# Values of four units multiplied together instead of two, with the maxima placed anew around them

## The reference

```python
def layer0(t):                      # t: (4, 1024, 768), normalised
    q, k, v = heads(t @ Wq + bq), heads(t @ Wk + bk), heads(t @ Wv + bv)
    attn = q @ k.T / 8 + rel_bias_h(q) + rel_bias_w(q)
    return (softmax(attn) @ v) @ Wp + bp
def layer1(t):                      # keys of the 7x7 neighbourhood only
    q, k, v = split(t @ qkv_w.T)
    return (softmax(q @ k[idx].T / 8) @ v[idx]) @ out_w.T
x = x + layer0(group_norm(x))
x = x + layer1(group_norm(x))
```

## Time and profile before

| | |
|---|---|
| median of three runs | 3558.11 us (3554.99 to 3559.51) |
| profiled execution | 3561.12 us, span 3558.6 us |
| PE busy | 3329.2 us, 94% |
| DVE, ACT, POOL busy | 46%, 34%, 30% |
| PE clock, mean granted | 0.989 of full |
| attention of the first image, layer 0 | 222 to 537 us of the span |
| attention of the first image, layer 1 | 782 to 857 us of the span |

### The profile page before, as it was taken

One profiled execution on the slowest core, in us unless ns is written; L12 is line 12 of the kernel. 1 busy time (PEld: TensorE's weight loads), 2 busy tenths in 40 slices (PEclk: granted clock), 3 DMA queues, 4 the chain that ended last, 5 costly groups with the idle time before them and its releaser, 6 DMA issues.

```text
span 3558.6 us, 49198 instructions
## 1 busy us (share of the span) xinstructions
PE 3329.2 (94%) x21388; PEld 2389.1 (67%) x21388; DVE 1639.5 (46%) x1497; ACT 1196.4 (34%) x1301; POOL 1083.5 (30%) x617
## 2 busy tenths in 40 slices
PE   6998899999999889999999888999989988899998
PEld 5864457786786455778678545587767854458776
DVE  4345545335434654543543465354354345534434
ACT  2334442124233444212333444321333244432132
POOL 0035671015003667002400366700330046660032
PEclk9999999999999999999999999999999999999999
DMA  2311003102321000310431100131143210013113
GB/s 98 107 30 22 16 13 124 45 28 89 134 92 36 19 13 24 114 43 28 133 117 66 35 18 14 33 110 36 34 148 101 69 27 19 19 36 112 36 31 104
DMA packets 158708, 210.94 MB, mean 59 GB/s; under 512 B 110496, under 2 KB 110752, under 8 KB 158496
## 3 DMA queue, kind: packets, MB, share of 16 engines
q1 hardware_dynamic: 158496, 207.81, 18.7%
HBM read 132.26 MB, written 50.33 MB: 51 GB/s over the span
## 4 chain that ended last, share of the span: by engine, by line
PE 69%; DVE 15%; issue 7%; ACT 5%; SPq 2%; DMA 2%; POOL 1%; ACTq 0%; DVEq 0%; POOLq 0%
PE score L909 14%; PE score L910 12%; PE score L911 12%; PE head_out L1038 7%; DVE max_part L687 6%; PE mx L973 6%; PE score L1008 5%; PE mx L976 3%; DVE recip L716 2%; SPq L343 2%; PE mx L991 2%; DVE o_raw L721 2%; PE score L1015 1%; ACT b_lo_raw L482 1%; DVE b_lo L707 1%
## 5 line engine op out<-in xcount | busy, mean ns | idle before, releaser
L440 POOL TENSOR_TENSOR acc<-acc,prob 128x1024 f32<-128x1024 f32 x288 | 721.1, 2527 | 245.7 <-ACT prob L578 245.6
L578 ACT ACTIVATE prob<-score 128x1024 f32<-128x1024 f32 (+3 forms) x576 | 514.7, 907 | 648.0 <-PE score L1021 550.0
L687 DVE TENSOR_REDUCE max_part<-mx 128x2 f32<-128x1024 f32 x384 | 467.6, 1218 | 423.8 <-PE mx L976 423.8
L1038 PE MATMUL head_out<-prob,v 128*64 128x512 f32 (+4 forms) x2496 | 491.5, 519 | 0.0
L909 PE MATMUL score<-a_hi,w_hi 128*128 128x512 f32 x1152 | 463.7, 403 | 25.7 <-DVE a_lo L677 10.0
L910 PE MATMUL score<-a_lo,w_hi 128*128 128x512 f32 x1152 | 451.8, 392 | 0.0
L911 PE MATMUL score<-a_hi,w_lo 128*128 128x512 f32 x1152 | 451.0, 391 | 0.0
L440 POOL TENSOR_TENSOR acc<-prob 128x1024 f32<-128x1024 f32 x48 | 113.3, 2381 | 969.7 <-ACT prob L578 782.5
L973 PE MATMUL mx<-k_hi,q_hi 64*128 64x512 f32 (+2 forms) x1152 | 266.0, 452 | 124.5 <-DVE max_part L687 109.3
L909 PE MATMUL score<-w_hi,a_hi 128*128 128x256 f32 x1152 | 346.3, 301 | 0.0
L973 PEld LDWEIGHTS mx<-k_hi,q_hi 64*128 64x128 f32 x1152 | 115.3, 185 | 317.3 <-issue 276.5
(11 more groups left out here) (106 smaller groups left out, 5435.6 us busy)
## 6 DMA issues: line engine op xcount, KB each, us to landing
raw<-weights SPq DMA_DIRECT2D x96, 768.0 KB, 4.2
g_mem<-g SPq DMA_DIRECT2D x24, 1024.0 KB, 4.6
recip<-recip SPq DMA_DIRECT2D x384, 64.0 KB, 2.0
xin<-x_t SPq DMA_DIRECT2D x24, 512.0 KB, 6.5
xr<-x_t SPq DMA_DIRECT2D x24, 512.0 KB, 5.0
x_mem<-xr SPq DMA_DIRECT2D x24, 512.0 KB, 6.9
xr<-x_mem SPq DMA_DIRECT2D x24, 512.0 KB, 6.3
y_t<-xr SPq DMA_DIRECT2D x24, 512.0 KB, 4.9
```

Source lines behind the costliest of these rows:

```text
L440: nc.gpsimd.tensor_tensor(acc[:, :, a:b], with_, now, ALU.add).then_inc(added, 1)
L578: nc.scalar.activation(prob[:, ug % P_SLOTS, :, 0:b - a], score[:, u % 2, :, 0:b - a], ACT.Exp, scale=SCALE).then_inc(prob_ok, 1)
L687: nc.vector.reduce_max(max_part[:, t, part, :], mx[:, :, 0:b - a], AX.X).then_inc(max_ok, 1)
L1038: last = nc.tensor.matmul(head_out[rows_of(h), half, x - half * HALF:y - half * HALF], v[:, t, p * 128 + 64 * h:p * 128 + 64 * h + 64], pr ...
```

## The change

Values are multiplied four units at a time, behind the second unit of the next four. The tables of maxima are written for single units: how many stand before a unit and how many behind it. `sums` stands behind the values of the last four units of the pair before, so `sums_copy` on ACT moves from behind unit 3 to behind unit 1. `invert` on DVE moves by one reduction. For the first pair all maxima and `shift` come by unit 15, and `bias_hi` moves behind it.

```diff
-MAXIMA = [(0, 1, 1), (0, 1, 1), (0, 1, 1), (1, 1, 1), (1, 1, 1), (1, 1, 1), (1, 0, 0), (0, 0, 0)]
-MAXIMA_FIRST = [(0, 0, 0), (0, 0, 0), (0, 1, 1), (1, 1, 1), (1, 1, 1), (1, 1, 1), (1, 1, 1), (1, 1, 0)]
+GROUPED = 4
+BEFORE = [1, 1, 0] + [1] * 11 + [0, 0]
+BEFORE_FIRST = [0] * 5 + [1] * 11
+BEHIND = [1, 5, 9]
+BEHIND_FIRST = [5, 9, 13, 15, 15]
...
+def shift_unit(layer, p):
+
+    return 5 if layer else 13 if p else 15
...
                         if u == 1 and p:
                             out_copy(f, p - 1)
-                        if u == 3 and p:
                             sums_copy(f, p - 1)
...
-                            if u == 14 and p + 1 < PAIRS:
+                            if u == (14 if p else 15) and p + 1 < PAIRS:
                                 bias_hi(f, p + 1)
...
-                        if p and k in (3, 4):
-                            invert(f, p - 1, k - 3)
+                        if p and k in (4, 5):
+                            invert(f, p - 1, k - 4)
...
+                def group_values(f, p, first):
+                    for u in range(first, first + GROUPED):
+                        values(f, p, u)
...
+                    ahead = layer == 0 and p + 1 < PAIRS
+                    for u in range(UNITS[layer]):
+                        if ahead:
+                            for _ in range(maxima_before(p, u)):
+                                maximum(f, p + 1, made)
+                                made += 1
+                        scores(f, p, u)
+                        if ahead:
+                            for _ in range(maxima_behind(p, u)):
+                                maximum(f, p + 1, made)
+                                made += 1
+                        if u % GROUPED == 1 and u > GROUPED:
+                            group_values(f, p, u - GROUPED - 1)
+                        elif u == 1 and p:
+                            group_values(f, p - 1, UNITS[layer] - GROUPED)
                             sums(f, p - 1)
-                        if p + 1 < PAIRS and step == shift_step(layer, p):
+                        if p + 1 < PAIRS and u == shift_unit(layer, p):
                             shift(f, p + 1)
```

More of the change, by code:

```diff
@@ L77, in max_at, with maxima_before, maxima_behind @@
     return k, 0, *key_span(k)
-MAXIMA = [(0, 1, 1), (0, 1, 1), (0, 1, 1), (1, 1, 1), (1, 1, 1), (1, 1, 1), (1, 0, 0), (0, 0, 0)]
-MAXIMA_FIRST = [(0, 0, 0), (0, 0, 0), (0, 1, 1), (1, 1, 1), (1, 1, 1), (1, 1, 1), (1, 1, 1), (1, 1, 0)]
[L86 to L92, removed]
+GROUPED = 4
[3 more added lines that the diff above has]
+BEHIND_FIRST = [5, 9, 13, 15, 15]
+def maxima_before(p, u):
+    return (BEFORE if p else BEFORE_FIRST)[u]
+def maxima_behind(p, u):
+    return (BEHIND if p else BEHIND_FIRST).count(u)
+def shift_unit(layer, p):
+    return 5 if layer else 13 if p else 15
 QK_MAX = [j * CT + i for j in range(8, TILES) for i in range(4)]
@@ L1149, in _ @@
                             sums(f, p - 1)
-                        if p + 1 < PAIRS and step == shift_step(layer, p):
+                        if p + 1 < PAIRS and u == shift_unit(layer, p):
                             shift(f, p + 1)
                 last_pair = PAIRS - 1
-                values(f, last_pair, UNITS[layer] - 2)
-                values(f, last_pair, UNITS[layer] - 1)
+                group_values(f, last_pair, UNITS[layer] - GROUPED)
                 def output(n, c):
```

## The result

The changed kernel takes 3679.39 us (median of 4 runs, 3677.6 to 3684.93), the kernel before beside it 3556.55 us. The ratio is 1.0349, with a 95% interval of 1.0336 to 1.0361: 123 us slower. The forecast was 3655 (3610 to 3700). One profile, that of values one at a time, is not read: in that execution (9806 us) TensorE's products took over twice their usual time at a granted clock of 1.000 (512 columns 1.00 us instead of 0.39), while the steps of DVE, ACT and POOL took what they always take.

The account below looks back on a forecast made before the run. PE, busy 94% of the span, was taken as the bound, through its products and waits. 3561.12 + 67 (layer 0) + 21 (layer 1) + 13 (clock) = 3662, as a median 3659, rounded to 3655; range 3610 to 3700.

Parts of the forecast that it names:

- Trips, 0.38 us: PE going over to values and back costs nearly 0.38 us; 144 fewer trips save 55 us if nothing else moved.
- Layer 0, forecast 67: Layer 0 loses 1.9 us in pair 0, 3.8 in pairs 1 to 3, 3.5 in pair 4; four images +67.
- The pair's start: Layer 0, pairs 1 to 3: first unit waits 2.2 us more for `bias_lo`, second maximum 0.9; together +2.6 a pair.
- `out_lo`: Layer 0, pairs 1 to 3: sixteenth maximum waits 3.1 us because `out_lo` waits for ACT; +0.7 a pair.
- `normalise`: Layer 0: only a unit of scores now covers this 2.71 us DVE step; eleventh maximum 2.2 us late, +0.9 a pair.
- Layer 1, forecast 21: POOL starts 2.7 us after `sums` and waits 0.9; sums to sums 13.7; weight copies add 1.3 in two pairs; +21.
- would give 13.0: Layer 1: PE's own work, instead of POOL's, would make a pair 13.0 us.
- The clock, forecast 13: Longer PE waits bring two more half-clock stretches an image, 1.6 us each; +13 over four images.
- five more an image, 32 us: Rival, chance 0.22 not its own but 0.17: clock takes over, five more half-clock stretches an image; 3678, up to 3700.
- The last pair, forecast 0: Layer 0, pair 5, without maxima: about 1.2 us gained, which disappears because the last `sums` waited for POOL anyway.
- The rival that trips are dear: Rival, chance 0.07: trips between the forms cost more than read, deciding from 1.1 us each, and the kernel gets faster.
- The rival that it cancels: Rival, chance 0.04: waits at the pair's start and `normalise` are covered by something moved along; within 0.2% of 3558.

Follow-up runs that it names:

- values one at a time: Against the kernel before: layer 0 multiplies one unit's values behind each unit of scores, DVE's long steps behind the last maxima; layer 1 unchanged. 3570.21 us (1.0035).
- the kernel kept busy: The changed kernel, with PE repeating the first product of the coming unit of scores ahead of its waits in layer 0, same result: 3631.57 us (1.0211).
- with POOL's start repaired: Against the kernel with only layer 1 grouped (3578.97): layer 1's sums back behind unit 3, grouped values left in place. 3565.98 us (1.0023).
- the repaired kernels: Changed kernel with pair start split, maxima re-placed, DVE's long steps later, layer 1 in twos: 3516.94 us; with layer 0's first pair also in twos: 3501.67.
- the old order with its steps late: The kernel before, values in twos, with normalise behind k = 14, out_hi behind unit 12 and out_lo behind k = 15: 3510.25 us (0.9872).
- moving three steps: The changed kernel with normalise moved behind k = 11, out_lo and weight_lo behind k = 15: 3589.91 us (1.0097).
- one number moved in the old order: The kernel before with out_lo behind k = 14 instead of k = 13: 3528.41 us (0.9924).

## Why the prediction was right

The direction, the range and the mechanisms held. The 123 us can be split by runs: half clock 48 (the kernel kept busy); layer 1 at full clock 6.0 × 4 = 24 (its stage takes 86.7 us there against 80.7); layer 0 the rest, 334.9 − 322.0 = 12.9 an image, 52. The sum is 124.

That split sets a kernel with hardly any half clock against one that has some. By the records of granted clock 75 us of the kernel before were at half clock, 198 of the changed one and 38 of the one kept busy. The last two differ by 160 us, which were worth 48, 0.3 each; so of the 123 us at half clock that the change added, an estimate is 37. Layer 0 then lost 123 − 24 − 37 = 62. Pairs that ran at full clock in both kernels bear it out: pair 3 is 54.9 us before and 58.1 in the kernel kept busy, +3.2 (forecast +3.8), pair 4 is 53.6 and 56.3, +2.7 (forecast +3.5). The forecast is compared with 62, 24 and 37.

- *Trips, 0.38 us.* The part inside a group is shown: 3.58 us for a group of sixteen, against 3.74. The steps around it are as they were read.
- *Layer 0, forecast 67, about 62 at equal clock.* The pair's start was right to 0.2 us in both its waits (2.01 and 0.73, forecast 2.2 and 0.9). `out_lo` was right to 0.1 us in pairs 1 to 3. **The term that was mis-sized is `normalise`**: "I get the eleventh maximum 2.2 us late". It was 3.51 − 2.13 = 1.4 us late, about what it had been before (3.37 − 2.16 = 1.2, which the forecast had as 1.3), so +0.1 to +0.2 and not +0.9 in each of 16 pairs, some 12 us. I had taken 9.3 us from the second inversion to `normalise` as the time until the transfers land; in the new order `normalise` started 427.19 − 418.67 = 8.5 us behind it, right behind a reduction and without a wait. 9.3 was one pair's distance, not the least. Some of the 12 us came back elsewhere, 3 of them in the last pair; where the rest did is not shown.
- *Layer 1, forecast 21, measured 24 at full clock, 28 as it ran.* The path over POOL was right to 0.1 us in each piece (2.76, 0.98 and 13.65; forecast 2.7, whose four parts as written make 2.6, 0.9 and 13.7). That PE's own side "would give 13.0" was near: with POOL's start repaired it is 12.9, so even then the saved trips do not bring it under the 12.77 of before.
- *The clock, forecast 13, about 37 added.* **This is the step that was most wrong.** I counted two more stretches of 3.4 us an image. The records of granted clock show 37.5 us at half clock in layer 0 of the first image, against 10.2 before, 27 more and not 7. Pairs 2 and 3 had 10 each: 6.8 from the wait at the start on (400.0 to 406.8 in pair 3) and 3.4 behind `out_lo`, most of it on work and not on waits. The forecast named "five more an image, 32 us" as a rival. There were eight more; the time that rival gave, 3678, is next to the 3679 measured, but with 67 for layer 0 and 32 for the clock.
- *The last pair, forecast 0*, is 54.3 us instead of 51.9; with the waits filled it is 52.6, so all but 0.7 was the clock.

Layer 0 came some 5 us under its forecast, layer 1 3 over and the clock 24 over. That the first is under is luck: had `normalise` cost what I wrote, the measured time would have been 12 us further off, at some 3691 of the 3700 that ended the range.

The rule of the Trainium skill that a change of tiling mode drains TensorE (TensorEngine Tiling (Array Packing), Key Properties), weighed in the forecast, agrees with the rows in sign: the steps into and out of a group are 0.1 us longer than plain ones. By the rows the saved changes are worth 55 us, an estimate, and more than that was lost elsewhere. The rival that trips are dear fell with the groups of 3.58 us and with the kernel getting slower. The rival that it cancels fell too: the waits were not covered. In the repaired kernels they are, and there the grouped order ends 9 us ahead of the old order with its steps late (3501.67 against 3510.25). That kernel keeps only a part of the saved changes: layer 1 and the first pair are in twos again, and the last four units of a pair are split.

## What to carry to other kernels

Work that holds the busiest engine without waiting for anybody (here the values) is the cover for everybody else's latency. Before grouping it to save switches, list each long step on the other engines and see that it stands right ahead of such a block, and that the block starts no later than the step; here moving three steps gave back 89 of 123 us, and one number moved in the old order was worth 28. With those steps moved in both, grouping itself was worth 9 us. Price a wait by more than its length: in pairs 2 and 3 here waits of 2 to 3 us on TensorE were followed by half clock for the work behind them. Not each was: pair 4, with a wait of 2.01 us at its start, stayed at full clock, and what decides it is not shown.

## What was not expected of the hardware

Adding 50 records of PE work to a pair of 61.6 us made it 58.0 us, since PEclk went from 0.92 to 1.00, and the whole kernel 48 us faster. Over the changed kernel PE's mean granted clock is 0.973, with its waits filled 0.995, above the 0.989 of the kernel before. The Trainium skill (TensorE: Matmul & The Clock Gate, What's actually happening) says that activity releases the throttle; this run agrees, and the activity may be a product whose result is overwritten.
